# Summing the counts of three destination tiles on VectorE before TensorE turns them

## The chip, the cores and the metric

The kernel runs on one core of a Trainium2 chip. The metric is the device time of one execution in microseconds, as a median over executions; lower is better. TensorE multiplies matrices, VectorE and ScalarE work elementwise, GpSimd (POOL in the profile) subtracts, and SyncE (SP) issues the DMA transfers.

## The reference, cut to what matters

Two graph layers act on 625 nodes of 1024 features, with 20,000 edges in 8 relations; each is followed by a residual and a layer normalization.

```python
# layer 0: attention over edges
h = x @ W
e = exp(-leaky_relu(al[src] + ar[dst]))
h_prime = segment_sum(e[:, None] * h[dst], src) / (segment_sum(e, src)[:, None] + EPS)
x = layernorm(x + elu(h_prime))
# layer 1: one mean and one matrix for each relation r, then a gate
u = x @ root + bias
for r in range(8):
    mask = (edge_type == r)
    sums = segment_sum(x[src] * mask[:, None], dst)
    cnt = segment_sum(mask, dst)
    u = u + (sums / maximum(cnt, 1)[:, None]) @ weight[r]
z = concatenate([u, x]) @ w_gate + b_gate
x = layernorm(x + (tanh(u) * z + x * (1 - z)))
```

The kernel replaces the walk over edges by a table of counts C[r][source][destination]: how many edges of relation r lead from a source to a destination. Layer 1 multiplies by C[r] of one relation at a time. Layer 0 needs no relation: for each pair it needs the number of edges of any relation, with the two axes swapped (turned).

## The kernel before, in words

Nodes are padded to 640, five tiles of 128. The order of all work is written out by hand, engine by engine; semaphores are its only coupling.

**The windows.** The counts are built in 40 windows of 16 destinations, so a destination tile j takes the eight windows 8j to 8j+7. The edges are sorted by destination, and a window covers one or two groups of five edge tiles of 128 edges. For each edge tile VectorE builds a one-hot row block `hot` (L761), and TensorE multiplies it with a one-hot of the sources (two matmuls, L993), which adds into two PSUM banks. There are four slots of `hot` for five edge tiles. So the builds of edge tiles 0, 1 and 2 of the next window run ahead, and that of edge tile 3 waits until TensorE has counted edge tile 0 of its own window. Both engines first read the bounds of a window from the tile `lohi_row` into registers (L281). TensorE opens a window with two small matmuls (L985) after ScalarE has copied the window before out of the banks, and closes it with two more (L998). ScalarE copies the window into `Cst[j % 2]` of shape 128 sources x 5 source tiles x 8 relations x 128 destinations (L491).

**Between the windows.** Behind the counts of window w, TensorE does pieces of other work: up to window 17 one or two `xw_item` of the product x @ W (three matmuls of 512 columns each, L927 to L929); then, from tile to tile, pieces of the attention product (`att_h`, L964 to L966) and `row_sums` (L972). VectorE does `drain_h` in windows 16 to 20 (three instructions that read a bank of the product, L724 and L726, ending in a wait for their own result), and for each tile j `leaky` (L737), `att_mult` (L743) and `att_low` (L748), spread over windows that `E_W` and `mult_w` name. ScalarE has the exponentials between them.

**The flush.** When the eight windows of tile j are copied, SyncE sends `Cst[j % 2]` to DRAM in five transfers of 512 KB (`flush(j)`, L306), for layer 1. The buffer is used again from window 8(j+2) on.

**The turn.** `turn_counts(j, part)` (L956) swaps the axes and sums over the relations at once: for each of the five source tiles, eight matmuls of 128x128 with the identity as the moving operand add into one PSUM block, 40 for a destination tile. Part 0 takes source tiles 0 to 3, part 1 takes source tile 4. For j from 0 to 3 TensorE does 16 of the matmuls in window 8j+8, 16 in window 8j+9 and 8 in window 8j+11; ScalarE copies the two parts out as int16 in windows 8j+10 and 8j+12 (`copy_turned`, L499). Tile 4 is turned behind the last window. `att_mult(j)` on VectorE needs both parts.

After the windows come the rest of the attention product, the normalization, and the long run of products of layer 1.

Of the kernel before, what the change touches and what calls it, by code (L numbers as in the profile page):

```python
# [5 lines left out]
def gat_rgcn_kernel(nc, dst_cols, src_cols, type_cols, dst_units, xT, x, weights, a, bias, b_gate, counts_dram, out):  # L6
# [51 lines left out]
    with ctx:  # L58
# [131 lines left out]
        counted = [sem(f"counted{s}") for s in range(BODY)]  # L190
        window_counted = sem("window_counted")
        window_copied = sem("window_copied")
        turned = sem("turned")
        turned_read = sem("turned_read")
        flushed = [sem(f"flushed{j}") for j in range(NT)]
# [72 lines left out]
        AL_W = DRAIN_FROM + NT  # L268
        E_W = [AL_W + 2, AL_W + 4, AL_W + 8, AL_W + 10, AL_W + 14]

        def mult_w(j):
            return max(E_W[j] + 3, PER * j + 13)

        def hp_w(j, t):
            return min(mult_w(j) + 3 + t, WINDOWS - 1)
# [172 lines left out]
        def _(act):  # L448
# [67 lines left out]
            for w in range(WINDOWS):  # L516
                copy_window(w)
                for k in range(RING, KT):
                    if w == SPLIT_AT[k]:
                        split_chunk(1, k)  # L520
                if SPREAD + 1 <= w < SPREAD + 1 + RING:
                    split_chunk(SEG_Z, w - SPREAD - 1)
                for j in range(NT - 1):
                    for part in range(2):
                        if w == PER * j + 10 + 2 * part:
                            copy_turned(j, part)
                if DRAIN_FROM - 1 <= w < DRAIN_FROM - 1 + NT:
                    copy_h(1, w - DRAIN_FROM + 1)
                if w == AL_W + 2:
                    act.wait_ge(al_ready, 1)  # L530
                    nc.scalar.copy(al_bc[:, :].rearrange("p (b n) -> p b n", b=2),
                                   pair(0).rearrange("p (b n) -> p b n", b=2)[:, :, 0:SPLIT]).then_inc(al_copied, 1)
                for j in range(NT):
                    if w == E_W[j]:
                        add_ar(j)
                for j in range(NT):
                    if w == E_W[j] + 2:
                        exp_e(j)
                for j in range(NT - 1):
                    if w == mult_w(j) + 1:  # L540
                        att_high(j)
# [94 lines left out]
        def _(dve):  # L636
# [95 lines left out]
            for k in range(RING):  # L732
                split_low(1, k)

            def leaky(j):
                dve.wait_ge(sum_done, j + 1)
                v.scalar_tensor_tensor(tmp[j % 2][:, :], tmp[j % 2][:, :], SLOPE, tmp[j % 2][:, :], ALU.mult, ALU.max)\  # L737
                 .then_inc(leaky_done, 1)
# [14 lines left out]
            for w in range(WINDOWS):  # L753
# [14 lines left out]
                if w == AL_W:  # L768
                    step(v.tensor_tensor(alr[:, :], dots[:, 0:2 * NT], dots[:, 2 * NT:4 * NT], ALU.add))
                    for t in range(NT):  # L770
                        d = v.tensor_scalar(diag[:, t * P:(t + 1) * P], ident, alr[:, t:t + 1], None, ALU.mult)
                    d.then_inc(diag_done, 1)
                for j in range(NT):
                    if w == E_W[j] + 1:
                        leaky(j)
# [131 lines left out]
        def _(pe):  # L907
# [38 lines left out]
            for i in range(EARLY):  # L946
                xw_item(1, *divmod(i, NT))

            def turn_counts(j, part, blocks=None):
                m0, m1 = turn_blocks(part)  # L950
                pe.wait_ge(window_copied, PER * (j + 1) + 1)
                if turn_bank(j, part) == 4:
                    pe.wait_ge(turned_read, 2 * j + part)
                for m in blocks or range(m0, m1):
                    for r in range(R):
                        last = mm(bank(turn_bank(j, part), c0=(m - m0) * P, c=P), Cst[j % 2][:, m, r, :], ident_r[:, :],  # L956
                                  start=r == 0, stop=r == R - 1)
                if m == m1 - 1:
                    last.then_inc(turned, 1)

# [20 lines left out]
            for w in range(WINDOWS):  # L981
# [18 lines left out]

                for k, t in items(w):
                    xw_item(1, k, t)
                for j in range(NT - 1):
                    for ahead, part, blocks in ((8, 0, (0, 1)), (9, 0, (2, 3)), (11, 1, (4,))):
                        if w == PER * j + ahead:
                            turn_counts(j, part, blocks)
# [186 lines left out]
```

## Time and profile before

| | |
|---|---|
| median of 3 runs | 1112.72 us (1111.9 to 1115.48) |
| the profiled execution | 1117.14 us, its span 1115.3 us |
| TensorE busy | 1040.4 us, 93% of the span |
| VectorE busy | 353.3 us, 32% |
| ScalarE, GpSimd busy | 264.0 us, 265.4 us, 24% each |

The profile is a record of one execution. Times in it count from the start of the span. The windows lie between 65.9 us and 219.9 us of it. "PE" is TensorE's matmuls, "PEld" its loads of the stationary operand, a "q" behind an engine (PEldq, DVEq) its sequencer, and a row of the timeline that reads "x10" is ten instructions in a row. Matmuls overlap, so a row of many lasts somewhat longer than the time until the next row can start.

### The profile page before, as it was taken

Reading aid. Unit: us, or ns where it says so; the run is one execution under the profiler, and the core shown is the slowest. Engines: PE = TensorE matmul, PEld = TensorE weight load, DVE = VectorE, ACT = ScalarE, POOL = GpSimd, SP = SyncE. Lnnn points to the kernel's source line nnn. Section 1 sums busy time; section 2 is a strip of 40 time slices with the busy share of each in tenths; the row PEclk is TensorE's granted clock in tenths of the full one; section 3 lists DMA queues with packets and bytes.
Section 4 is the critical chain, followed back from the end, with each engine's and each line's share of the span. In section 5 each row is a group of like instructions: output and inputs, shape, how many; then the busy total and the mean of one; then the engine's idle time right before and its main releaser. Section 6 shows DMA issues by size and latency. Waiting matters only on the chain.

```text
span 1115.3 us, 14888 instructions
## 1 busy us (share of the span) xinstructions
PE 1040.4 (93%) x5432; PEld 861.0 (77%) x5432; DVE 353.3 (32%) x698; ACT 264.0 (24%) x452; POOL 265.4 (24%) x201
## 2 busy tenths in 40 slices
PE   5699878896999999999999999999999999999977
PEld 3455545585788889889889889889889889888855
DVE  7954566446111022022022022022012012112277
ACT  3212234345111121121121121122121122222320
POOL 0000000103532222222222312321311321327480
PEclk9989989998999999999999999999999999999988
DMA  6113323425622132132131131131141141212212
GB/s 207 48 57 114 95 58 87 153 80 191 179 79 64 38 108 65 39 115 59 38 121 52 38 123 51 38 125 48 38 135 39 38 135 38 76 48 66 76 39 92
DMA packets 63621, 91.81 MB, mean 82 GB/s; under 512 B 4115, under 2 KB 30178, under 8 KB 63428
## 3 DMA queue, kind: packets, MB, share of 16 engines
q1 hardware_dynamic: 63556, 90.86, 25.8%
q8 instruction: 51, 0.84, 0.3%
q14 instruction: 14, 0.11, 0.0%
HBM read 75.17 MB, written 15.67 MB: 81 GB/s over the span
## 4 chain that ended last, share of the span: by engine, by line
PE 83%; DVE 7%; POOL 3%; issue 2%; ACT 1%; DVEq 1%; POOLq 0%; ACTq 0%
PE ps L927 17%; PE ps L928 17%; PE ps L929 17%; PE ps L1098 9%; PE ps L1099 9%; PE ps L993 4%; PE ps L1087 2%; PE ps L956 2%; DVE hot L761 2%; POOL x_lo L420 1%; PE ps L1147 1%; POOL u L405 1%; PE ps L1148 1%; PE ps L1149 1%; DVE oh_s L699 1%
## 5 line engine op out<-in xcount | busy, mean ns | idle before, releaser
L393 POOL TENSOR_TENSOR w_lo<-w_raw,w_hi 128x512 fp32r<-128x512 f32 x168 | 215.3, 1285 | 771.0 <-ACT w_hi L459 553.6
L927 PE MATMUL ps<-w_hi,M_hi 128*128 128x512 f32 (+1 forms) x560 | 223.5, 399 | 17.7 <-DVE w_lo L694 11.4
L459 ACT CAST w_hi<-w_raw 128x512 fp32r<-128x512 f32 x184 | 114.2, 622 | 480.0 <-PE ps L929 415.3
L928 PE MATMUL ps<-w_hi,M_lo 128*128 128x512 f32 (+1 forms) x560 | 220.3, 393 | 0.0
L929 PE MATMUL ps<-w_lo,M_hi 128*128 128x512 f32 (+1 forms) x560 | 220.2, 393 | 0.0
L842 DVE SCALAR_TENSOR_TENSOR u<-ps,scale,u 128x512 f32<-128x512 f32 (+1 forms) x90 | 66.4, 744 | 423.1 <-PE ps L929 423.1
L1098 PE MATMUL ps<-C_hi,x_hi 128*128 128x320 f32 (+3 forms) x640 | 193.1, 319 | 0.0
L1099 PE MATMUL ps<-C_hi,x_lo 128*128 128x320 f32 (+3 forms) x640 | 192.0, 317 | 0.0
L927 PE MATMUL ps<-w_hi,M 128*128 128x512 f32 (+1 forms) x360 | 140.5, 390 | 0.0
L929 PE MATMUL ps<-w_lo,M 128*128 128x512 f32 (+1 forms) x360 | 140.5, 390 | 0.0
L928 PE MATMUL ps<-w_hi,M 128*128 128x512 f32 (+1 forms) x360 | 140.4, 390 | 0.0
L927 PEld LDWEIGHTS ps<-w_hi,M_hi 128*128 128x128 f32 (+1 forms) x560 | 105.1, 188 | 43.2 <-DVE w_lo L694 13.6
L1099 PEld LDWEIGHTS ps<-C_hi,x_lo 128*128 128x128 f32 (+1 forms) x640 | 127.5, 199 | 0.3
L1098 PEld LDWEIGHTS ps<-C_hi,x_hi 128*128 128x128 f32 (+1 forms) x640 | 127.3, 199 | 0.4
L929 PEld LDWEIGHTS ps<-w_lo,M_hi 128*128 128x128 f32 (+1 forms) x560 | 105.0, 188 | 23.7
L928 PEld LDWEIGHTS ps<-w_hi,M_lo 128*128 128x128 f32 (+1 forms) x560 | 105.3, 188 | 22.4
L761 DVE TENSOR_SCALAR hot<-table,key 128x640 bf16<-128x640 f16 x210 | 69.9, 383 | 70.1 <-PE ps L993 53.9
L993 PE MATMUL ps<-hot,oh_s 128*128 128x320 bf16 x420 | 76.0, 313 | 13.3 <-DVE hot L761 6.3
L929 PEld LDWEIGHTS ps<-w_lo,M 128*128 128x128 f32 (+1 forms) x360 | 66.7, 185 | 14.9
L928 PEld LDWEIGHTS ps<-w_hi,M 128*128 128x128 f32 (+1 forms) x360 | 66.8, 186 | 14.6
L927 PEld LDWEIGHTS ps<-w_hi,M 128*128 128x128 f32 (+1 forms) x360 | 66.8, 185 | 14.5
L993 PEld LDWEIGHTS ps<-hot,oh_s 128*128 x420 | 31.0, 99 | 46.4 <-issue 39.1
(140 smaller groups left out, 768.8 us busy)
## 6 DMA issues: line engine op xcount, KB each, us to landing
w_raw<-weights SPq DMA_DIRECT2D x192, 256.0 KB, 2.9
C_dram<-Cst SPq DMA_DIRECT2D x25, 512.0 KB, 5.9
C_hi<-C_dram SPq DMA_DIRECT2D x8, 1600.0 KB, 6.9
z<-b_gate SPq DMA_DIRECT2D x5, 512.0 KB, 9.6
u<-bias SPq DMA_DIRECT2D x5, 512.0 KB, 8.5
xT_raw<-xT SPq DMA_DIRECT2D x8, 312.5 KB, 7.5
u<-x SPq DMA_DIRECT2D x4, 512.0 KB, 5.0
out<-u SPq DMA_DIRECT2D x4, 512.0 KB
```

The lines of the kernel that those rows point to most:

```text
L393: pool.tensor_tensor(w_lo[k % RING][:, :], w_raw[k % RING][:, :], w_hi[k % RING][:, :].bitcast(f32), ALU.subtract).then_inc(w_lo_done, 1)
L459: nc.scalar.copy(w_hi[k % RING][:, :], w_raw[k % RING][:, :]).then_inc(w_hi_done, 1)
L761: v.tensor_scalar(hot[:, SLOT[s] * NP:(SLOT[s] + 1) * NP], table[:, :], float(WIN * w), key[:, ds(tile + s, 1)], ALU.add, ALU.is_equal).th ...
L842: v.scalar_tensor_tensor(u[r, t, half * H2:(half + 1) * H2], bank(t, rows(t)), scale[odd][r, t:t + 1], u[r, t, half * H2:(half + 1) * H2], ...
L927: mm(o, lhs_hi[:, k, c], w_hi[k % RING][:, :], start=opens, stop=False)
L928: mm(o, lhs_lo[:, k, c], w_hi[k % RING][:, :], start=False, stop=False)
L929: last = mm(o, lhs_hi[:, k, c], w_lo[k % RING][:, :], start=False, stop=closes_)
L956: last = mm(bank(turn_bank(j, part), c0=(m - m0) * P, c=P), Cst[j % 2][:, m, r, :], ident_r[:, :], start=r == 0, stop=r == R - 1)
L993: last = mm(bank(5 + c, c=SPLIT), oh_s[:, ds(edge + s * P, P)], hot[:, SLOT[s] * NP + c * SPLIT:SLOT[s] * NP + (c + 1) * SPLIT], start=Fal ...
L1087: last = mm(bank(5, c0=2 * t, c=2), C_hi[:, m, t * P:(t + 1) * P], ones_r[:, 0:2], start=m == 0, stop=m == NT - 1)
L1098: mm(o, x1_hi[r, m, f], C_hi[r, m, c0:c0 + cn], start=m == 0, stop=False)
L1099: last = mm(o, x1_lo[r, m, f], C_hi[r, m, c0:c0 + cn], start=False, stop=m == NT - 1)
```

## The change

For destination tiles 0, 1 and 2, VectorE sums the eight relations of `Cst[j % 2]` in place, in three steps (`fold`): relations 0 to 3 plus 4 to 7 (2560 elements in each partition), then 0 and 1 plus 2 and 3 (1280), then 0 plus 1 (640). The folds stand in windows 8j+11, 8j+12 and 8j+13, one in each, behind that window's builds and `drain_h` and ahead of its `leaky`, `att_mult` and `att_low`. The first waits until the flush of the tile has landed, since it overwrites what the flush reads. TensorE then turns only relation 0: four matmuls in window 8j+14 and one in window 8j+15, in place of the 40. ScalarE copies the parts out in the same windows as TensorE turns them. Tiles 3 and 4 stay as they were. `mult_w`, the window of `att_mult`, comes out at 26, 28, 32 and 37 with both forms.

```diff
+        summed = sem("summed")
...
+        FOLDED = 3
+        FOLDS = 3
+        FOLD_W = PER + 3
+
+        def turn_w(j, part):
+            return PER * j + FOLD_W + FOLDS + part if j < FOLDED else PER * j + PER + 2 + 2 * part
+
         def mult_w(j):
-            return max(E_W[j] + 3, PER * j + 13)
+            return max(E_W[j] + 3, turn_w(j, 1) + 1)
...
-                        if w == PER * j + 10 + 2 * part:
+                        if w == turn_w(j, part):
                             copy_turned(j, part)
...
+            def fold(j, f):
+                n = R >> (f + 1)
+                C = Cst[j % 2]
+                if f == 0:
+                    dve.wait_ge(flushed[j], 16 * NT)
+                else:
+                    dve.wait_ge(summed, FOLDS * j + f)
+                v.tensor_tensor(C[:, :, 0:n, :], C[:, :, 0:n, :].bitcast(f32), C[:, :, n:2 * n, :].bitcast(f32), ALU.add)\
+                 .then_inc(summed, 1)
...
+                for j in range(FOLDED):
+                    for f in range(FOLDS):
+                        if w == PER * j + FOLD_W + f:
+                            fold(j, f)
...
-            def turn_counts(j, part, blocks=None):
+            def turn_counts(j, part, blocks=None, rounds=R):
                 m0, m1 = turn_blocks(part)
                 pe.wait_ge(window_copied, PER * (j + 1) + 1)
+                if rounds < R:
+                    pe.wait_ge(summed, FOLDS * (j + 1))
                 if turn_bank(j, part) == 4:
                     pe.wait_ge(turned_read, 2 * j + part)
                 for m in blocks or range(m0, m1):
-                    for r in range(R):
+                    for r in range(rounds):
                         last = mm(bank(turn_bank(j, part), c0=(m - m0) * P, c=P), Cst[j % 2][:, m, r, :], ident_r[:, :],
-                                  start=r == 0, stop=r == R - 1)
+                                  start=r == 0, stop=r == rounds - 1)
...
-                for j in range(NT - 1):
+                for j in range(FOLDED):
+                    for part in range(2):
+                        if w == turn_w(j, part):
+                            turn_counts(j, part, rounds=1)
+                for j in range(FOLDED, NT - 1):
                     for ahead, part, blocks in ((8, 0, (0, 1)), (9, 0, (2, 3)), (11, 1, (4,))):
```

## Rows read from the trace of the kernel before

**Rows 1.** Page: the chain that ended last, its share by engine
```profile
PE 83%; DVE 7%; POOL 3%; issue 2%; ACT 1%; DVEq 1%; POOLq 0%; ACTq 0%
```
**Rows 2.** The chain in order of time, 60 to 262 us, by line
```profile
by line: PE ps L993 23.7%; PE ps L956 9.9%; DVE hot L761 8.4%; issue 7.7%; PE ps L927 5.2%; PE ps L928 4.3%; PE ps L929 4.2%; PE ps L964 3.4%; DVE stats L799 3.2%; DVE u L797 3.1%; DVE gt L796 3.0%; PE ps L966 3.0%; PE ps L965 2.9%; PE ps L
```
**Rows 3.** Timeline of PE around tile 0's turn: start us, us, engine, line
```profile
95.33 0.19 PE L998 MATMUL ps<-zeros 128*128 128x2 bf16 x2
...
96.84 1.90 PE L956 MATMUL ps<-ident,Cst 128*128 128x128 f32 x16
...
98.65 1.85 PE L993 MATMUL ps<-hot,oh_s 128*128 128x320 bf16 x10
100.33 0.19 PE L998 MATMUL ps<-zeros 128*128 128x2 bf16 x2
...
112.59 1.85 PE L993 MATMUL ps<-hot,oh_s 128*128 128x320 bf16 x10
...
115.61 1.86 PE L993 MATMUL ps<-hot,oh_s 128*128 128x320 bf16 x10
```
**Rows 4.** Line L281, register loads: ns min/median/max, first and last start us
```profile
L281 PEldq TENSOR_LOAD <-lohi_row x40: 532/538/1968, 62.0 to 216.7; - x40
...
L281 PEldq TENSOR_LOAD <-lohi_row x1: 1779/1779/1779, 96.4 to 96.4; - x1
...
L281 PEldq TENSOR_LOAD <-lohi_row x1: 1807/1807/1807, 100.7 to 100.7; - x1
...
L281 PEldq TENSOR_LOAD <-lohi_row x1: 1867/1867/1867, 162.9 to 162.9; - x1
```
**Rows 5.** Timeline of DVE, builds of edge tiles 3 and 4, windows 11 and 12
```profile
109.08 0.68 DVE L761 TENSOR_SCALAR hot<-table,key 128x640 bf16<-128x640 f16 x2 [1.09 <-PE ps L993]
...
113.18 0.68 DVE L761 TENSOR_SCALAR hot<-table,key 128x640 bf16<-128x640 f16 x2 [1.91 <-PE ps L993]
```
**Rows 6.** Groups by form, 120 to 340 us: two fp32 operations of two tensors
```profile
L796 DVE SCALAR_TENSOR_TENSOR gt<-et,gt 128x1024 f32<-128x1024 f32 x4 | 4.9, 1214 | 3.4 <-ACT gt L555 3.4
...
L748 DVE TENSOR_TENSOR M_lo<-tmp,M_hi 128x640 fp32r<-128x640 f32 x5 | 4.1, 821 | 0.8 <-ACT M_hi L514 0.8
```
**Rows 7.** Timeline of DVE in windows 19 to 22
```profile
143.31 0.68 DVE L726 TENSOR_TENSOR M<-ps,M 128x512 fp32r<-128x512 f32 x1
144.93 1.80 DVE L761 TENSOR_SCALAR hot<-table,key 128x640 bf16<-128x640 f16 x5 [0.93 <-DVE M L726]
...
147.87 0.69 DVE L726 TENSOR_TENSOR M<-ps,M 113x512 fp32r<-113x512 f32 x1
149.50 1.81 DVE L761 TENSOR_SCALAR hot<-table,key 128x640 bf16<-128x640 f16 x5 [0.94 <-DVE M L726]
...
152.40 0.97 DVE L761 TENSOR_SCALAR hot<-table,key 128x640 bf16<-128x640 f16 x3
```
**Rows 8.** Timeline of DVE in windows 27 and 28
```profile
172.28 1.80 DVE L761 TENSOR_SCALAR hot<-table,key 128x640 bf16<-128x640 f16 x5
...
177.98 0.82 DVE L748 TENSOR_TENSOR M_lo<-tmp,M_hi 128x640 fp32r<-128x640 f32 x1
178.71 1.80 DVE L761 TENSOR_SCALAR hot<-table,key 128x640 bf16<-128x640 f16 x5
```
**Rows 9.** Timeline of PE, counts of windows 21, 22 and 28
```profile
150.03 2.59 PE L993 MATMUL ps<-hot,oh_s 128*128 128x320 bf16 x10 [1.68 <-DVE hot L761]
...
153.78 2.85 PE L993 MATMUL ps<-hot,oh_s 128*128 128x320 bf16 x10
...
175.83 2.08 PE L993 MATMUL ps<-hot,oh_s 128*128 128x320 bf16 x10
```
**Rows 10.** Windows of 2 us: busy of PE, PEld, DVE, ACT, POOL; PEclk, DMA share, GB/s
```profile
148.00:150.00 2.00, 0.20 (x2) 0.11 (x2) 1.06 (x3) 0.78 (x3) 0.00 (x0) 1.00 0.00 0
150.00:152.00 2.00, 1.97 (x9) 1.00 (x10) 1.82 (x8) 0.00 (x0) 0.00 (x0) 0.59 0.00 0
...
172.00:174.00 2.00, 1.31 (x9) 0.54 (x10) 1.85 (x6) 0.74 (x2) 0.00 (x0) 1.00 0.01 1
```

## The prediction

> **What bounds the kernel now.** I read the page's chain first: TensorE carries 83% of the time, VectorE 7% [rows 1]. That is an average over stages, so I followed the chain in order of time through the stage that the change touches. There the turn (L956) holds 9.9% of 202 us, some 20 us for 200 matmuls, or 4 us for each destination tile; but the builds of `hot` (L761) stand in the same chain with 8.4% [rows 2]. In every window TensorE hands over to VectorE and back: the build of edge tile 3 starts 0.59 us after TensorE begins to count (112.59 to 113.18), and a count starts 0.53 us after the build it needs has begun (149.50 to 150.03) [rows 3, 5, 7, 9]. The reader should see in this that VectorE's idle time there is the other half of a handshake. What is put into it delays the builds behind it. Then I read the two timelines window by window, and the register loads of the sequencers, to see for each removed piece what ends last once it is gone. Everything behind the windows waits for their end, so I take a delay there one to one.
>
> **The price of a fold.** No in-place sum of this size is in the trace. The nearest rows are fp32 operations of two tensors in SBUF: 821 ns for 640 elements and 1214 ns for 1024, which is 1.02 ns for each further element [rows 6]. By that the folds of 2560, 1280 and 640 elements last 2.79, 1.48 and 0.82 us. The next instruction starts about 0.09 us before such a row ends (177.98 + 0.82 against 178.71) [rows 8]. So they take 2.70, 1.39 and 0.74 us of VectorE's time, 4.8 us a tile and 14.5 us in all. From below: an instruction can't be freer of overhead than the slope alone, 2.62 + 1.31 + 0.66 = 4.6 us a tile. From above: three rows' full lengths, 5.1 us a tile. That is at most 0.3 us a tile either way. In the same way two builds take 0.60 us (0.68 less 0.08) and five in a row 1.72 us.
>
> **Tile 0.** Removed: 16 matmuls in window 8 (from 96.84 to the opening just ahead of 98.65, 1.74 us), 16 in window 9, 8 in window 11 (0.87). But the matmuls of window 8 lie over a second thing. TensorE's sequencer must read the bounds of window 9, and while the flush fills the DMA queues that read lasts 1.78 us instead of 0.54 [rows 4]. It began at 96.4, late because the sequencer first issued the turn; the count had closed at 95.33 [rows 3]. With no turn to issue I let it begin there: it ends at 97.1, the opening follows, and the count some 0.4 behind it, at 97.6 in place of 98.65. Saved: 1.0, not 1.74. In window 9 the read began at 100.7 behind a close at 100.33, and lasts 1.81 [rows 3, 4]; saved: 0.35. Together 1.35 us.
>
> Fold 0 waits for the flush, which has long landed (the loads of L281 in the next windows are fast again). It stands behind the builds of window 11: 109.08 + 0.60 + 2.70 = 112.38, only then the builds for window 12, and the count at 112.91 instead of 112.59 [rows 3, 5]. So with the 0.87 us of turn gone the count still comes 0.3 late. Fold 1: 112.91 + 0.59 + 0.60 + 1.39 + 0.53 = 116.02 against 115.61, 0.4 late in all [rows 3]. Fold 2 is half as long and the window has two items of the product behind it; nothing. Added: five matmuls in windows 14 and 15 at 0.11 us each (16 in 1.74), 0.55, on the path since TensorE runs through there. Tile 0: -1.35 + 0.4 + 0.55 = **-0.4 us**.
>
> **Tile 1.** Its turn stood in windows 16, 17 and 19, where `drain_h` on VectorE sets the pace and TensorE waits for a build afterwards. Removed there: nothing gained. Added: fold 0 behind the `drain_h` of window 19. That ends at 143.31 + 0.61 = 143.92; the fold runs from about 144.0 to 146.70, and the builds of window 20 start then instead of at 144.93, 1.77 late. It is not the full 2.70, since the 0.93 us of the sequencer's own wait and register load now run beside the fold [rows 7]. Window 20 in the same way: 148.55 + 1.39 = 149.94 against 149.50, 0.44 more. Fold 2 moves the builds for window 22 from 152.40 to 153.14, so a count could start at 153.67; it started at 153.78, so this one is just covered [rows 7, 9]. Four matmuls in window 22 stand ahead of the broadcast of al: 0.44; that in window 23 lies under ScalarE's copy. Tile 1: 1.77 + 0.44 + 0.44 = **+2.65 us**.
>
> **Tile 2.** The turns of windows 24 and 25 look like 3.7 us of saving. The register loads take it: that of window 24 begins at 162.9, 0.1 us behind the close of the count, and lasts 1.87; that of window 25 begins 0.3 behind its close and is the longest of the 40, 1.97 [rows 4]. They last as long as the 16 matmuls beside them. Saved: 0.4 for both. The 8 in window 27 lie over ScalarE's copy; saved: nothing. Fold 0 stands behind the five builds of window 27: 172.28 + 1.72 + 2.70 = 176.70, the count at 177.23 instead of 175.83 [rows 8, 9]. In window 28 VectorE also has `att_mult(1)` and `att_low(0)` and was already what TensorE waited for: 176.70 + 1.72 + 1.39 + 2 x 0.74 = 181.29 for the next builds instead of 178.71, 2.58 late in all [rows 8]. Fold 2 in window 29 ends at 181.29 + 1.72 + 0.74 = 183.75, while TensorE is busy with that window's count and the attention product until about 185; covered. The flush of this tile is over before: at 172 to 174 the DMA queues are at 0.01 [rows 10]. Should it land late, the fold waits, behind it all builds, and behind them TensorE, one to one. Added: five matmuls, 0.55. Tile 2: -0.4 + 2.58 + 0.55 = **+2.7 us**.
>
> ScalarE's copies out move by four windows but are as many and as long, and `att_mult` has its old windows; I cost them at nothing. If a copy came late, `add_ar` in window 23 would be 0.3 late, which the long load of window 24 hides.
>
> The handshake sum is -0.4 + 2.65 + 2.7 = +4.95 us.
>
> **TensorE's clock.** After a stretch with 0.20 us of matmuls in 2 us the granted clock fell from 1.00 to 0.59, that is towards 1.2 GHz [rows 10], and ten matmuls took 2.59 and 2.85 us instead of 1.86 [rows 3, 9]; I put such a stretch at (2.59 - 1.86) + (2.85 - 1.86), and 0.8 for the broadcast in it, 2.5 us. The change makes more such idle: 2.8 us of it ahead of window 29, and a longer one ahead of window 20. Bounds: nothing if no further fall comes, 5.0 for two more. I take half a stretch, 1.25 us. The Trainium skill, "TensorE: Matmul & The Clock Gate", "Why this matters for your kernels", says that idle gaps between bursts of matmuls put the array back to its low clock; by that rule the gap ahead of window 29 alone would cost its stretch, and the sum would be 7.5 us (case C below goes further). The trace agrees that such gaps are what precedes the falls.
>
> The sum against the profiled execution is 1117.14 + 6.2 = 1123.3; that execution lies 4.4 us above the median of the runs shown. Against the median: 1112.72 + 6.2 = **1118.9 us**, 0.6% slower. 0.3% (3.3 us) is about what a measurement of this kernel can tell from no change.
>
> **Rivals.** (A) *The register loads shrink.* Without the turns TensorE's loads may fall elsewhere or end sooner than 1.8 us. Against it: all four long ones lie in the flush, which stays. If they were as short as the median 0.54 [rows 4], windows 8, 9, 24 and 25 would give back some 3 us more: 1112.7 + 4.95 - 3 = 1114.7, no change within what can be told. [...] (B) *VectorE's slack swallows the folds and the turns come off the chain in full*, the mechanism that makes it faster: three fifths of 20 us, less an eighth, is 10.5 us [rows 2]; 1102.2. For it speaks that VectorE is idle half of the time there; against it the handshake in every window and `drain_h`. It decides in the windows 11 and 27: if the count behind fold 0 starts no later after the one before it than it did, this holds. Faster by 0.3% would need the folds and loads to take less than 7.2 of the 10.5. (C) *The clock falls twice more*, at both tiles: 4.95 + 5.0, and with longer folds 10.5; 1123. The idle stretches speak for it; the fall at the second one is uncertain.
>
> **Numbers.** Forecast (1116.3 to 1121.5) 0.58; A 0.20; B 0.08; C 0.14. Within the forecast and A, some of the chance lies on each side of 0.3%. Faster 0.09, same 0.22, slower 0.69. The range holds the forecast, C, and most of A: 1112.8 to 1123.5; B is left out.
>
> **What would show it.** Nine L-rows of the fold, near 2.8, 1.5 and 0.8 us. The count of window 12 some 4.4 us behind that of window 11, against 4.1 now, though the turn is gone. The builds of window 20 about 2.7 us behind the end of `drain_h`'s last row instead of 0.9. The count of window 29 some 4.6 us behind that of window 28 instead of 3.4. TensorE's loads still 1.8 us in windows 8, 9, 24 and 25. A granted clock below 1 near window 29. The prediction is wrong if the folds are much shorter than their rows, if TensorE's loads no longer follow the flush, or if the clock, which falls twice in windows 19 to 22 now, is left high there.

## The result and the profile after

| | before | after |
|---|---|---|
| median | 1112.31 us (1111.55 to 1115.48) | 1126.79 us (1122.79 to 1130.39) |
| ratio | | 1.0128 [1.0097, 1.0160] |

Run again on another occasion (the first experiment), it was 1124.39 against 1112.52 us, 1.0100 [1.0075, 1.0125]. So the change costs 11 to 14 us: slower, as forecast, and about twice the 6.2 us of the sum, outside the range. The profiled execution took 1122.79 us. Its span and its chain by engine, from the page:

```profile
span 1120.8 us, 14686 instructions
...
PE 81%; DVE 7%; issue 4%; POOL 3%; ACT 1%; DVEq 1%; POOLq 0%; ACTq 0%
```

TensorE's share fell from 83% to 81%, VectorE's stayed at 7%, and "issue", where nothing in the profile holds the engine, went from 2% to 4% [rows 1]. Most of that growth lies in the stage that the change touches. The chain from 60 to 262 us, by line:

```profile
by line: PE ps L1017 22.8%; issue 13.0%; DVE hot L779 9.7%; PE ps L980 5.7%; PE ps L949 4.2%; PE ps L950 3.5%; PE ps L951 3.5%; PE ps L988 3.4%; DVE gt L818 3.0%; PE ps L990 3.0%; PE ps L989 2.9%; DVE M_lo L732 2.9%; DVE stats L821 2.6%; PE
```

The turn is down from 9.9% to 5.7% of 202 us, 8.5 us less, but "issue" is up from 7.7% to 13.0%, 10.7 us more [rows 2]: among it are the register loads, which the turns used to cover.

The prices of the folds, groups by form, 100 to 190 us (sum us, mean ns of one, idle before):

```profile
L750 DVE TENSOR_TENSOR Cst<-Cst 128x2560 fp32r<-128x2560 f32 x3 | 8.5, 2821 | 0.0
L750 DVE TENSOR_TENSOR Cst<-Cst 128x1280 fp32r<-128x1280 f32 x3 | 4.5, 1488 | 0.0
L750 DVE TENSOR_TENSOR Cst<-Cst 128x640 fp32r<-128x640 f32 x3 | 2.5, 822 | 0.0
```

Against 2.79, 1.48 and 0.82 us, worked out from [rows 6]. TensorE's register loads of windows 8, 9, 24 and 25:

```profile
L289 PEldq TENSOR_LOAD <-lohi_row x1: 1796/1796/1796, 94.3 to 94.3; - x1
...
L289 PEldq TENSOR_LOAD <-lohi_row x1: 1929/1929/1929, 98.3 to 98.3; - x1
...
L289 PEldq TENSOR_LOAD <-lohi_row x1: 1865/1865/1865, 164.6 to 164.6; - x1
...
L289 PEldq TENSOR_LOAD <-lohi_row x1: 1918/1918/1918, 168.7 to 168.7; - x1
```

They are as long as before [rows 4], with no turn beside them, so the turns didn't make them long; the flush runs at that time (the DMA share is 0.99 to 1.08 from 94 to 102 us). The timeline of TensorE, counts of windows 9 to 12, of window 20, and of windows 27 to 29:

```profile
96.57 1.86 PE L1017 MATMUL ps<-hot,oh_s 128*128 128x320 bf16 x10 [0.18 <-issue]
...
100.61 1.86 PE L1017 MATMUL ps<-hot,oh_s 128*128 128x320 bf16 x10 [0.18 <-issue]
...
106.13 1.85 PE L1017 MATMUL ps<-hot,oh_s 128*128 128x320 bf16 x10
...
110.56 1.86 PE L1017 MATMUL ps<-hot,oh_s 128*128 128x320 bf16 x10 [1.01 <-DVE hot L779]
...
145.75 2.85 PE L1017 MATMUL ps<-hot,oh_s 128*128 128x320 bf16 x10 [2.78 <-DVE hot L779]
...
174.34 2.84 PE L1017 MATMUL ps<-hot,oh_s 128*128 128x320 bf16 x10
...
179.06 2.85 PE L1017 MATMUL ps<-hot,oh_s 128*128 128x320 bf16 x10 [0.83 <-DVE hot L779]
...
183.91 1.86 PE L1017 MATMUL ps<-hot,oh_s 128*128 128x320 bf16 x10 [0.98 <-DVE hot L779]
```

And VectorE's, the fold of window 11, the one of window 19, and the first of tile 2:

```profile
107.31 2.82 DVE L750 TENSOR_TENSOR Cst<-Cst 128x2560 fp32r<-128x2560 f32 x1
110.04 1.80 DVE L779 TENSOR_SCALAR hot<-table,key 128x640 bf16<-128x640 f16 x5
...
141.77 0.69 DVE L734 TENSOR_TENSOR M<-ps,M 128x512 fp32r<-128x512 f32 x1
142.49 2.83 DVE L750 TENSOR_TENSOR Cst<-Cst 128x2560 fp32r<-128x2560 f32 x1
145.23 0.97 DVE L779 TENSOR_SCALAR hot<-table,key 128x640 bf16<-128x640 f16 x3
...
175.80 2.82 DVE L750 TENSOR_TENSOR Cst<-Cst 128x2560 fp32r<-128x2560 f32 x1
```

Read the two together: each fold ends just as the builds start (107.31 + 2.82 against 110.04; 142.49 + 2.83 against 145.23), and TensorE counts 0.52 us behind that start. The count of window 12 comes 4.43 us after that of window 11 (forecast 4.4), the builds of window 20 come 2.77 us behind `drain_h`'s last row (141.77 + 0.69 to 145.23; forecast 2.7), the count of window 29 comes 4.85 us after that of window 28 (forecast 4.6). The ten matmuls of windows 20, 27 and 28 take 2.85 us instead of 1.86. Stretches of 2 us around windows 27 and 28 (columns as in [rows 10]):

```profile
172.00:174.00 2.00, 1.08 (x6) 0.59 (x6) 2.00 (x5) 0.69 (x1) 0.00 (x0) 0.59 0.32 94
174.00:176.00 2.00, 1.87 (x9) 1.04 (x10) 1.43 (x6) 0.00 (x0) 0.00 (x0) 0.50 0.00 0
176.00:178.00 2.00, 1.22 (x7) 0.65 (x5) 2.00 (x1) 0.73 (x2) 0.00 (x0) 0.50 0.02 4
...
180.00:182.00 2.00, 1.94 (x10) 1.01 (x7) 2.00 (x4) 0.02 (x1) 0.00 (x0) 0.50 0.00 0
182.00:184.00 2.00, 0.29 (x3) 0.21 (x4) 2.00 (x6) 0.68 (x1) 0.00 (x0) 0.85 0.00 0
```

The granted clock is at 0.50, that is 1.2 GHz, for 10.2 us, from about 172.4 to 182.6.

To place the rest I cut each execution in two: the **windows**, from ScalarE's copy of window 7 to that of window 39, and the **tail**, from there to the end of the span. The table below gives both for every run. "After", the changed kernel, has 133.9 and 895.6 us. The kernel before has 127.6 and 895.4 in its first profile, and 126.6 and 889.6 in a second one. Against the second, only 7.3 us (5.5 in a repeat of after) of the 11 to 14 lie in the windows; the rest is in the tail, whose work the change doesn't touch. Against the first, from which the sum was worked out, the windows are 6.3 us longer and the tail is the same.

### The profile page after: what moved, and what is told of

Its sections match the earlier page's. It is cut to its first block, busy times and chain, and to the rows that moved or that the text cites. A ratio compares the mean times of both kernels' runs of the same rounds, so it can differ in the third digit from the quotient of the medians.

```text
span 1120.8 us, 14686 instructions
## 1 busy us (share of the span) xinstructions
PE 1032.9 (92%) x5327; PEld 848.7 (76%) x5327; DVE 367.7 (33%) x707; ACT 264.5 (24%) x452; POOL 265.6 (24%) x201
## 4 chain that ended last, share of the span: by engine, by line
PE 81%; DVE 7%; issue 4%; POOL 3%; ACT 1%; DVEq 1%; POOLq 0%; ACTq 0%
PE ps L949 17%; PE ps L951 17%; PE ps L950 17%; PE ps L1126 9%; PE ps L1127 9%; PE ps L1017 4%; PE ps L1115 2%; DVE hot L779 2%; POOL x_lo L428 1%; PE ps L980 1%; POOL u L413 1%; PE ps L1175 1%; PE ps L1176 1%; PE ps L1177 1%; DVE oh_s L707 1%
## 5 line engine op out<-in xcount | busy, mean ns | idle before, releaser
L1126 PEld LDWEIGHTS ps<-C_hi,x_hi 128*128 128x128 f32 (+1 forms) x640 | 126.3, 197 | 0.4
L1017 PE MATMUL ps<-hot,oh_s 128*128 128x320 bf16 x420 | 79.2, 325 | 19.8 <-DVE hot L779 13.3
```

The lines of the kernel that those rows point to most:

```text
L1017: last = mm(bank(5 + c, c=SPLIT), oh_s[:, ds(edge + s * P, P)], hot[:, SLOT[s] * NP + c * SPLIT:SLOT[s] * NP + (c + 1) * SPLIT], start=Fal ...
L1126: mm(o, x1_hi[r, m, f], C_hi[r, m, c0:c0 + cn], start=m == 0, stop=False)
```

## The experiments

Every ratio is to the kernel before, timed beside it on the same chip. Windows and tail (us) are of each run's one profiled execution; the clock is the mean granted TensorE clock over a whole execution, the median of the runs.

| run | median us | ratio to before | windows | tail | clock |
|---|---|---|---|---|---|
| f1_before (one execution) | 1109.86 | | 126.6 | 889.6 | 0.977 |
| e1_again | 1124.39 | 1.0100 [1.0075, 1.0125] | 132.1 | 899.0 | 0.963 |
| e2_turn_less | 1117.75 | 1.0041 [1.0024, 1.0059] | 128.2 | 899.0 | 0.966 |
| e3_folds_only | 1121.21 | 1.0068 [1.0043, 1.0093] | 133.3 | 893.7 | 0.967 |
| e4_fold_one | 1112.77 | 0.9996 [0.9976, 1.0017] | 126.5 | 893.3 | 0.971 |
| f2_after_filled | 1126.84 | 1.0141 [1.0100, 1.0182] | 131.8 | 901.8 | 0.970 |
| f3_less_filled | 1118.54 | 1.0059 [1.0035, 1.0082] | 125.1 | 898.7 | 0.974 |
| f4_before_filled | 1123.54 | 1.0110 [1.0081, 1.0139] | 125.3 | 902.3 | 0.971 |
| g1_delay_1us | 1115.08 | 1.0032 [1.0013, 1.0051] | 127.8 | 895.6 | 0.973 |
| g2_delay_2us | 1117.04 | 1.0038 [1.0016, 1.0059] | 126.3 | 896.8 | 0.970 |
| g3_before_spread | 1105.11 | 0.9936 [0.9915, 0.9958] | 126.5 | 883.2 | 0.981 |
| g4_after_spread | 1114.77 | 1.0028 [1.0010, 1.0047] | 134.9 | 888.6 | 0.972 |
| h1_before_pad | 1120.08 | 1.0081 [1.0061, 1.0100] | 127.2 | 896.1 | 0.970 |
| h2_after_pad | 1120.79 | 1.0086 [1.0069, 1.0104] | 134.9 | 892.4 | 0.966 |
| h3_after_spread_pad | 1112.60 | 1.0011 [0.9997, 1.0024] | 135.9 | 887.2 | 0.975 |
| h4_less_spread_pad | 1106.23 | 0.9960 [0.9946, 0.9974] | 128.2 | 884.0 | 0.975 |
| i1_folds_spread | 1114.30 | 1.0008 [0.9993, 1.0023] | 133.6 | 886.9 | 0.973 |
| i2_before_spread | 1104.07 | 0.9935 [0.9910, 0.9961] | 126.6 | 883.7 | 0.982 |

**Which half of the change costs.** The changed kernel again; the changed kernel without its folds (layer 0 then takes its counts from relation 0 alone); the kernel before with the folds added and their result unused (the third piece of its turn, and ScalarE's copy of the first part, moved one window ahead, so that the buffer is free); and the change for one tile alone.

```diff
 # e2_turn_less, against after
-                for j in range(FOLDED):
-                    for f in range(FOLDS):
-                        if w == PER * j + FOLD_W + f:
-                            fold(j, f)
...
-                if rounds < R:
-                    pe.wait_ge(summed, FOLDS * (j + 1))
 # e3_folds_only, against before: the folds of after, and
-                    for ahead, part, blocks in ((8, 0, (0, 1)), (9, 0, (2, 3)), (11, 1, (4,))):
+                    for ahead, part, blocks in ((8, 0, (0, 1)), (9, 0, (2, 3)), (10, 1, (4,))):
 # e4_fold_one, against after
-        FOLDED = 3
+        FOLDED = 1
```

> The changed kernel once more. Theory 1 (the handshake in the windows is the whole cost, 6 us, and the executions timed so far were drawn high): about 1118 us, ratio 1.005 to 1.006. Theory 2 (a second cost of some 7 us exists that comes in part of the executions and that the first trace of the change did not catch): two clusters again, near 1123 and near 1130, ratio 1.010 to 1.016, and a trace from the upper cluster is some 7 us longer at one place behind or inside the windows.

> The changed kernel without the folds and the wait for them, so that relation 0 alone is turned and layer 0 gets its counts alone: the removal by itself. Theory 1 (handshake): 1.35 us saved in windows 8 and 9, 0.8 in window 11, 0.4 in windows 24 and 25, against some 1.5 us of new matmuls: -1 us, 1111.3. Theory 2a (the idle that the removal leaves on TensorE lowers its clock, and that is the second cost): slower than before by 3 to 8 us, 1115 to 1120. Theory 2b (the second cost needs the folds): as theory 1.

> The kernel before with the nine folds added behind its full turn of 40 matmuls for each tile; the third piece of the turn moves from window 8j+11 to 8j+10, the copy of part 0 from 8j+10 to 8j+9, and the folded result is not used. Theory 1 (handshake): tile 0 +1.2, tile 1 +2.2, tile 2 +2.6, in all +6 us, 1118.3. Theory 2a (the second cost comes with the missing turns): again +6. Theory 2b (the second cost needs the folds alone): +12 to +15 us, 1124 to 1127.

> The changed kernel with tile 0 alone folded (FOLDED = 1); tiles 1 and 2 are turned as before. Theory 1 (handshake): -0.4 us, 1111.9, the same as before. A cost in proportion to the number of folded tiles: a third of 14.5 us, 1117. Theory 2 with the second cost at tiles 1 and 2, where TensorE's clock falls: -0.4 us.

The removal alone, which takes 105 matmuls away, made the kernel slower by 0.4%, with windows of 128.2 us (1.7 more than in the second trace of before) and a tail of 899.0. The folds alone cost 0.7%, and their windows are about as long as those of the full change (133.3). One tile alone made no difference that can be told, which fits the sum's -0.4 us for tile 0. So most of what lies in the windows comes with the folds, and something else, which came with fewer matmuls too, lengthens the tail.

The two halves don't simply add, though. From window 23 to 32 after is 3.7 us slower than the second trace of before, and the removal alone, without any fold, 3.6. Stretches of 2 us in the removal alone (e2):

```profile
164.00:166.00 2.00, 0.16 (x5) 0.10 (x4) 0.55 (x2) 1.81 (x3) 0.00 (x0) 1.00 1.00 280
...
168.00:170.00 2.00, 1.08 (x8) 0.62 (x7) 1.98 (x5) 0.69 (x1) 0.00 (x0) 0.50 0.03 8
170.00:172.00 2.00, 2.00 (x9) 1.11 (x8) 0.69 (x3) 0.00 (x0) 0.00 (x0) 0.50 0.00 0
```

Where the turns of tile 2 stood beside the register loads, which still take 1.86 and 1.93 us, TensorE is now idle (0.16 us of matmuls in 2), and the granted clock is below 1.00 for 13.7 us behind it. With this idle time filled (next experiment) the same nine windows are only 1.5 us slower. So the removal gains nothing there and loses something: the loads last as long without the turns, and the clock falls behind them.

**The clock in the windows.** Identity matmuls into a bank that nobody reads give TensorE work in its idle gaps, in the kernel before, in after, and in the removal alone. The kernel before was also traced a second time.

```diff
+                if w in FILL:
+                    pe.wait_ge(u_drained, 2 * NT + 1)
...
+                    for _ in range(FILL[w]):
+                        mm(bank(0, c=P), ident_r[:, :], ident_r[:, :], start=True, stop=True)
 # before: FILL = {18: 16, 20: 16}
 # after, and the removal alone: 12 to 16 in windows 16 to 20, 24, 25, 27 and 28
```

> The kernel before once more, for a trace beside the first. Clock theory (the executions of before have fewer stretches at 1.2 GHz in the windows than its first trace, which was the slowest execution of four, shows): fewer than 10.2 us at half clock between 138 and 158 us, window 39 copied earlier than 219.9. Rival (the added time lies in the folds and is complete in the first pair of traces): the windows end where they did, within 1 us of 219.9.

> The changed kernel, with matmuls of the identity with itself in the idle of TensorE (16 of 128x128 behind the counts of windows 16, 18, 19, 20 and 28, 12 in 17 and 27, 14 in 24 and 25), written to a PSUM bank that nobody reads. They add 13 us of busy time and no result. Clock theory (the missing turns and the longer waits lower TensorE's clock, and that is what the sum of the prediction lacked): faster than the changed kernel in spite of the added work, 1117 to 1120 with the handshake's 5 to 6 us left. Rival (folds delay the builds by more than I counted, the clock costs nothing): 1124 or, with the fill in the way, 1125 to 1127.

> The changed kernel without the folds (relation 0 alone is turned, layer 0 gets its counts alone), with the same fill. Without the fill it took 1117.75. Clock theory: 1111 to 1113, what the handshake sum gave for the removal. Rival (the removal costs by the new place of the five matmuls and the copies, not by the clock): stays at 1117 to 1119.

> The kernel before, with 16 such matmuls behind the counts of windows 18 and 20, where TensorE waits for drain_h on VectorE. Clock theory: the fall that some executions have there goes, 0 to 3 us faster than before, 1109.5 to 1112.5. Rival: no difference, or up to 0.5 us slower if the fill delays the opening of a window.

The filled after, same stretch as above, in pieces of 2 us, and TensorE's counts of windows 27 to 29:

```profile
174.00:176.00 2.00, 1.62 (x11) 0.63 (x12) 1.86 (x6) 0.00 (x0) 0.00 (x0) 1.00 0.00 0
176.00:178.00 2.00, 1.71 (x18) 1.59 (x16) 2.00 (x1) 1.77 (x3) 0.00 (x0) 1.00 0.01 4
```

```profile
174.29 1.86 PE L1018 MATMUL ps<-hot,oh_s 128*128 128x320 bf16 x10 [0.30 <-DVE hot L780]
...
178.74 1.86 PE L1018 MATMUL ps<-hot,oh_s 128*128 128x320 bf16 x10 [1.03 <-DVE hot L780]
...
183.32 1.86 PE L1018 MATMUL ps<-hot,oh_s 128*128 128x320 bf16 x10 [0.78 <-DVE hot L780]
```

With the clock at 1.00 the counts take 1.86 us, and still stand 4.45 and 4.58 us apart: what is left is the handshake. The windows of the filled after are 5.24 us longer than those of the second trace of before (131.82 against 126.58), against +4.95 in the sum; both traces have one stretch below 1.00 in the windows, 6.8 us long, from about 146 to 155. The removal alone, filled, has no such stretch: its windows are 1.44 us shorter than those of the unfilled kernel before and 0.2 us shorter than those of the filled one (125.34), which has none either; the expectation was about -1. So the handshake sum is near in all, and the rest of the windows' length, 0.3 to 2 us in after and its repeat, goes with the clock.

But no median improved, and all three expectations missed: 1126.84 for 1117 to 1120, 1118.54 for 1111 to 1113, 1123.54 for 1109.5 to 1112.5. The kernel before with 32 matmuls in its gaps had windows 1.2 us shorter and came out 1.1% slower, all of it in the tail (902.3 against 889.6 us). That ruled out a tail that merely starts later.

**A pure delay.** Eight or sixteen identity matmuls, 0.87 and 1.74 us, right behind the last window of the kernel before:

```diff
+            pe.wait_ge(turned_read, 2 * E)
+            for _ in range(8):
+                mm(bank(4, c=P), ident_r[:, :], ident_r[:, :], start=True, stop=True)
```

> The kernel before with 8 matmuls of the identity (0.87 us) put in front of the turn of tile 4, behind the last window; nobody reads them. New theory (the relation steps fall to the lower clock or not according to the moment at which they begin; eight times in a row): far more than 0.87 us, about 1118 (+5 to +8), and a run behind the windows of some 896 to 900 us instead of 890 to 893. Theory of the prediction (a delay counts one to one): 1113.3.

> The same with 16 (1.74 us). New theory: about 1120 to 1123 (+8 to +10), as the traces with such late ends of the windows have 899 to 902 us behind them. One to one: 1114.1.

0.87 us cost 3.4 us (1115.08 against 1111.69; by the interval 1.4 to 5.7), 1.74 us cost 4.2 us by the ratio (1.8 to 6.6) and 5.4 by the medians. That is more than one to one, clearly for the first and barely for the second, and less than the 5 to 8 and 8 to 10 us that I had expected. The edits also lengthen TensorE's program by 16 and 32 instructions. So one microsecond ahead of the tail need not be one microsecond of the total.

Where the tail loses time: each of layer 1's eight relation steps has 25 matmuls of two columns for the degrees. In the second trace of the kernel before, the timeline and the stretches around one such block:

```profile
430.19 2.95 PE L1087 MATMUL ps<-ones_r,C_hi 128*128 128x2 f32 x25
```

```profile
430.00:432.00 2.00, 2.00 (x19) 1.96 (x18) 0.00 (x0) 0.62 (x1) 0.92 (x1) 1.00 0.41 135
432.00:434.00 2.00, 2.00 (x14) 2.00 (x14) 0.36 (x2) 0.00 (x0) 0.34 (x1) 0.70 0.19 31
434.00:436.00 2.00, 2.00 (x9) 2.00 (x9) 0.00 (x0) 0.00 (x0) 0.00 (x0) 0.50 0.30 100
```

TensorE is 100% busy in the row sense, and the granted clock falls from 1.00 to 0.50, so that 9 matmuls pass in 2 us instead of some 16. Over the fourteen traces that have the block, the fall, where it comes, begins 2.0 to 4.3 us after the start of the block, near its end or just behind it, and lasts some 3.5 us. In this execution it comes at every second block, four of eight; in the first trace of the kernel before at seven, in after at six, in its repeat at all eight. From the start of one block to the start of the next, a step without the loop's jump back takes 80.3 us without a fall and 81.8 with one, in every trace: a fall costs 1.5 us (a stretch twice as long costs 3.1). In the filled kernel before it looks the same:

```profile
518.00:520.00 2.00, 2.00 (x18) 2.00 (x18) 0.18 (x2) 0.00 (x0) 1.06 (x1) 0.93 0.00 1
520.00:522.00 2.00, 2.00 (x9) 2.00 (x9) 0.17 (x1) 0.00 (x0) 0.00 (x0) 0.50 0.41 131
```

**Spreading the degree matmuls.** The same 25, five each behind the last five items of the product before them, in the kernel before, in after, and in the folds alone:

```diff
                         if degrees is not None and k == KT - 1:
                             degree_sums(degrees, t)
...
-            def aggregate(i, half):
-
-                if half == 0:
+            def degree_sums(i, t):
+                if t == 0:
...
-                    for t in range(NT):
-                        for m in range(NT):
-                            last = mm(bank(5, c0=2 * t, c=2), C_hi[:, m, t * P:(t + 1) * P], ones_r[:, 0:2],
-                                      start=m == 0, stop=m == NT - 1)
+                for m in range(NT):
+                    last = mm(bank(5, c0=2 * t, c=2), C_hi[:, m, t * P:(t + 1) * P], ones_r[:, 0:2],
+                              start=m == 0, stop=m == NT - 1)
...
```

> The kernel before with one edit in the relation step: the 25 two-column matmuls of the degrees (3 us in a row ahead of the aggregation) are put behind the five last items of the product that runs before, five behind each. New theory: the falls of the clock in the steps go, each step takes 81.8 us or less, the time falls to 1104 to 1109 and scatters less. Rival (the falls come from something else in the step): no change, 1112.5.

> The changed kernel with the same edit. New theory: the change then costs only what the windows show, 4.5 to 7 us against the kernel before with the edit. Rival (the second cost is not in the steps): the distance stays 12 us.

> The folds alone on top of the full turns (as in the earlier run of the folds alone), with the degree sums spread. The handshake sum for this form is +6.0 us with no offset from removed turns. With the clock of the windows 0 to 2 more: 1111 to 1113 against 1105 for the kernel before with the spread. Rival (most of the folds' measured 8.7 us was the steps): 1108 to 1110.

> The kernel before with the degree sums spread, on the same chip as the run beside it: 1105 again, 0.993 to 0.995 of the kernel before.

The kernel before with the block spread (i2), one of its pieces of five and the stretches around it:

```profile
428.53 0.61 PE L1087 MATMUL ps<-ones_r,C_hi 128*128 128x2 f32 x5
```

```profile
430.00:432.00 2.00, 2.00 (x14) 1.79 (x14) 0.00 (x0) 0.00 (x0) 0.00 (x0) 1.00 0.44 131
432.00:434.00 2.00, 2.00 (x16) 1.92 (x15) 0.36 (x2) 0.62 (x1) 0.84 (x1) 1.00 0.00 0
434.00:436.00 2.00, 2.00 (x17) 2.00 (x16) 1.06 (x2) 0.53 (x2) 0.46 (x1) 1.00 0.15 29
```

The clock stays at 1.00 throughout, and the tail is 883.2 and 883.7 us in place of 889.6: 6 us for four falls, 1.5 each. From 400 to 900 us the clock doesn't leave 1.00 in any of the six traces with the block spread. The kernel before gains 0.65% by it, after 0.7 to 1.0%, so the falls at the blocks would be 1 to 4 us of what the change cost; the intervals of the lower figure allow nothing as well. And the expectation for after missed: with the block spread in both kernels the change still costs 9.7 us (1114.77 against 1105.11), not 4.5 to 7. The folds alone cost 8.2 us by the ratios (1.0008 against 0.9935) and 10.2 by the medians, no less than without the spread (7.6 and 8.7), though 6 to 8 was expected.

**Where TensorE's code lies.** The change takes 105 matmuls out of TensorE's program, 210 instructions. TensorE's wait list of after (engine, line, waited for: us in total, times, longest), 300 to 960 us; its second row has none like it in the kernel before:

```profile
PE ps L949 <- DVE M_lo L877: 4.0, 3, 1.5
PE ps L949 <- issue: 1.7, 2, 1.3
```

The loop over the relations has two steps in its body and jumps back three times. The waits for `M_lo` stand right behind the jumps; the "issue" gaps stand 4.5 to 6.4 us further on, behind two or all three of them. I saw such gaps in the kernels with 210 instructions less than before (after, its repeat, e2, g4; 1.7 to 2.8 us in all) and in those with 54 to 64 more (the three filled ones; 4.4 to 5.4), and in none of the others. So I changed the length alone, with matmuls of two columns on zeros at TensorE's start: 26 (52 instructions) in the kernel before, 80 in after, in after with the block spread, and in the removal alone with the block spread.

```diff
+            pe.wait_ge(dve_step, 1)
+            for _ in range(26):
+                mm(bank(6, c=2), zeros[:, :], zeros[:, 0:2], start=True, stop=True)
```

> The kernel before with 26 two-column matmuls on zeros (52 instructions) at the very start of TensorE's program, where it waits for VectorE. Code-place theory: a second gap of 0.5 to 2 us at each of the three jumps back of the relation loop, 2 to 5 us in all, and the time at 1114 to 1117. Rival (the gap belongs to the missing turns or to the fill): no gap, 1111.7.

> The changed kernel with 80 such matmuls (160 instructions) at the start, 5 to 8 us of narrow work inside TensorE's first wait. Code-place theory: the second gap goes, 1119 to 1122 against 1124 to 1127. Rival: 1124 to 1127, or longer by what the padding itself delays (under 1 us).

> The changed kernel with the degree sums spread and the same 160 instructions. Code-place theory: 2 to 3 us faster than without them (1114.8), so 1111.5 to 1113, and then 6 to 8 us above the kernel before with the spread (1105.1), which is what the windows show. Rival: 1114.8.

> The removal alone (no folds; relation 0 alone is turned, layer 0 gets its counts alone), with the spread and the padding. If the 5 us that the removal alone cost were the steps and the code's place: 1104 to 1107, within 2 us of the kernel before with the spread (1105.1). Rival (the removal costs by itself in the windows): 1109 or more.

The same list for the padded kernel before, and two rows of its timeline behind one jump:

```profile
PE ps L930 <- DVE M_lo L855: 3.6, 3, 1.3
PE ps L932 <- issue: 2.1, 2, 1.6
```

```profile
487.47 0.49 PE L930 MATMUL ps<-w_hi,M_hi 128*128 128x512 f32 x1 [1.31 <-DVE M_lo L855]
...
493.23 0.50 PE L932 MATMUL ps<-w_lo,M_hi 128*128 128x512 f32 x1 [1.60 <-issue]
```

And for the padded after, which has no row of issue there:

```profile
PE ps L952 <- DVE M_lo L877: 4.4, 3, 1.5
```

Fifty-two idle instructions made the kernel before 9 us slower (1120.08 against 1110.47, 1.0081 [1.0061, 1.0100]), above the 1114 to 1117 expected; up to 0.6 us of it is a later start of the windows (92.5 against 91.9 us). After with 160 more instructions was at 1.0086 [1.0069, 1.0104], below its two ratios without them (1.0128 and 1.0100), by intervals that overlap with theirs; with the block spread it was at 1.0011 against 1.0028, intervals that overlap as well. That the gaps come and go with the length of the program ahead of the loop is shown by the traces. How much of the change's loss they are is an estimate, 2 to 5 us by these medians, 1.7 and 1.9 us by the gaps in the traces of after and its repeat.

**Both together.** The number of falls at the eight blocks and the sum of the issue gaps, for each trace with the tail beside it:

| trace | tail | falls | issue gaps, us |
|---|---|---|---|
| f1_before | 889.6 | 4 | 0 |
| before, first trace | 895.4 | 7 | 0 |
| h2_after_pad | 892.4 | 5 | 0 |
| g1_delay_1us | 895.6 | 6, one twice as long | 0 |
| after | 895.6 | 6 | 1.7 |
| h1_before_pad | 896.1 | 6 | 2.1 |
| e1_again | 899.0 | 8 | 1.9 |
| e2_turn_less | 899.0 | 7 | 2.6 |
| f3_less_filled | 898.7 | 6 | 4.5 |
| f2_after_filled | 901.8 | 8 | 4.4 |
| f4_before_filled | 902.3 | 7, one twice as long | 5.4 |
| g3, h4, i2 (spread) | 883.2 to 884.0 | 0 | 0 |
| g4_after_spread | 888.6 | 0 | 2.8 |

Take 883.4 us, 1.5 for each fall (3.1 for one twice as long) and the gaps, and each of these tails comes out right within 2.5 us, nearly always a little too short. In the five traces left (e3, e4, g2, h3, i1) 3.5 to 7.4 us are missing; they have a further stretch at the low clock, ahead of the steps, between 224 and 242 us. So in these traces the tail is longer by falls of the clock and by the gaps, in the padded and the filled kernels too. What decides how many falls there are isn't shown: two executions of the kernel before have four and seven.

Why the place matters is argued, not shown. The Trainium skill, "Runtime: NRT & Kernel Launch", "Instruction fetch mechanics", says that an engine's instructions are fetched in blocks of 16 KiB, 256 instructions, and that a taken branch into a block that isn't held makes the engine wait. The trace agrees with the size: in after the queue of instructions moved 0.82 MB in 50 packets, 16 KB each:

```profile
q8 instruction: 50, 0.82, 0.3%
```

And the lengths agree with the distance: -210 and +46 are 256 apart, and the gaps were there at -210 and at +52 to +64, and absent at -70, -50, 0, +16 and +32. Which jump misses which block no run shows.

## Why the prediction was wrong, step by step

**What failed.** The step "Everything behind the windows waits for their end, so I take a delay there one to one". It is a sentence about order, and the order is right; the conclusion is not. It put what the change does to the tail at nothing more than its later start. Against the second trace of the kernel before the tail is 6.0 us longer in after and 9.4 in its repeat. Of the 6.0, two more falls of the clock at the degree blocks are 3.0 us and the issue gaps 1.7; of the 9.4, four more falls are 6.0 and the gaps 1.9. The gaps depend on how many instructions TensorE's program has ahead of the loop. The delay of 0.87 us that cost 3.4 (1.4 to 5.7) points the same way. With the blocks spread in both kernels and after's length moved out of the gaps, the change costs 1.0011 / 0.9936, 0.75% or 8.4 us (two ratios of different occasions). The other 3 to 6 us of the 11 to 14 are then the tail's; medians can't part the two causes, since their intervals are as wide as the parts.

**Luck.** Held against the execution from which it was worked out, the forecast seems right: 1123.3 against the 1122.79 us of after's profiled execution, and windows 6.3 us longer against a sum of 6.2. But that execution of the kernel before, at 1117.14 us, was slower than all four timed in the table above, with seven falls and a tail of 895.4 us, as long as after's. From the second trace, with four falls, the same sum gives 1109.86 + 6.2 = 1116.1, 6.7 us below it.

**The handshake sum was near, in part by offsets.** +4.95 forecast, +5.24 in the filled after against the second trace of the kernel before. By stages: windows 8 to 16, -0.8 (forecast -0.4); 16 to 23, +3.3 (2.65); 23 to 32, +3.2 (2.7); the last seven -0.5 (nothing). So two stages were 0.5 to 0.7 too low and the others made up for it. Without the fill after has -0.6, +4.4, +3.7 and -0.3. The folds' prices came within 0.03 us, and the register loads kept their 1.8 us. The removal was worth little, as the loads had it: -0.2 to -1.4 us with the idle time filled, for matmuls that hold some 12 us of the chain [rows 2].

**The clock's term was too small.** +1.25 forecast; the windows of the unfilled runs with the whole change are 5.5 to 9.3 us longer than those of the second trace of before, so the clock's part is about 0.3 to 4, within the bounds of nothing to 5.0. The prediction looked for further falls where the folds make TensorE wait, ahead of windows 20 and 29. It took the bare register loads of windows 24 and 25 only for a saving that doesn't come; in after TensorE idles 1.86 and 1.83 us there, and the 10.2 us below 1.00 that follow come in the removal alone too, 13.7 us long.

**A reading that was wrong.** "All four long ones lie in the flush": the trace of the kernel before has eight register loads above 1 us on TensorE. The other four start at 128.0 (1.89 us), 133.8 (1.11), 193.4 (1.78) and 198.0 (1.56), also while the DMA share is high (0.81 to 1.02 where they start). It changes no term of the sum.

**The rivals.** (A) fell: the loads didn't shrink. (B) fell: the count of window 12 stands 4.43 us behind that of window 11, more than before. (C) gives a total within 4 us of the measured one, but puts it all in the windows.

**What stays open.** What decides at which blocks the clock falls, and whether it falls between 224 and 242 us; the median of a kernel moves with both. Why the padded kernel before lost 9 us: its one trace has 2.1 us of gaps and two more falls than the second trace of before, 5.1 us together, but that the gaps bring the falls wasn't shown. The removal alone, at its best place, is at 0.9960, the kernel before with the block spread at 0.9936; its windows (128.2) are 1.6 us longer, so there 105 fewer matmuls gain nothing.

**The best version** is the kernel before with the degree matmuls spread, 1104.07 us and 1105.11, 0.9935 [0.9910, 0.9961] and 0.9936 [0.9915, 0.9958]. Neither the folds nor the removal improves it.

## What to carry to other kernels

Before you take work off the busiest engine, find what ends last once it is gone: here a register load, a drain or a copy lay under nearly all of it, while most of what was put on the partner of the handshake came through. Ask too what the bare wait does to TensorE's clock. Then don't take a delay ahead of a long tail one to one: look in the trace for falls of the granted clock and "issue" gaps in the tail, in more than one execution, and measure what moves them with a pure delay and a pure padding, two kernels of three lines each. A change of under 1% can be less than what moving a loop by 50 instructions does.

## What the runs showed of the hardware that I had not expected

- At a block of 25 matmuls of two columns, 2.9 us in a row and 100% busy, the granted clock falls from 1.00 to 0.50 in some steps, for some 3.5 us, which costs 1.5 us of time. Spread in fives of 0.61 us there was no fall from 400 to 900 us, and the kernel was 0.65% faster. The Trainium skill, "TensorE: Matmul & The Clock Gate", "Why this matters for your kernels", names idle gaps between bursts as what drops the clock; in the rows of PE there was none here.
- A delay of 0.87 us ahead of eight such steps cost 3.4 us (1.4 to 5.7).
- 52 instructions that do nothing useful, ahead of a loop, cost 9 us of 1110, with gaps of 1.6 and 0.5 us behind two of the loop's jumps.
- Register loads of 0.53 us take 1.1 to 2.0 us while the DMA share is 0.8 or more.
- An in-place sum of fp32 in SBUF takes 822, 1488 and 2821 ns for 640, 1280 and 2560 elements in each partition, 1.04 ns for each further element.
